# Four edits to a decoder kernel: a later load order in the second cross attention, causal rows scaled on ScalarE, a rotation-table wait moved, a zero fill issued in stage 1

## The reference, cut to what matters

```
x = layernorm(x + L0 self attention(x))             # 64 heads of 8, q, k, v with bias
x = layernorm(x + L0 cross attention(x, ctx))
x = layernorm(x + L0 mixture of experts(x))         # top 2 of 8 experts, on a latent of 256
x = layernorm(x + L1 causal attention(x))           # 16 heads of 128, 4 key/value heads, rotation
x = layernorm(x + L1 cross attention(x, ctx, pos))  # 32 heads of 16, rotation by position
x = layernorm(x + L1 ternary feed-forward(x))
def _layernorm(x, axis=-1, eps=1e-05):
    return (x - mean(x)) / sqrt(var(x) + eps)
```

## Time and profile before

| | us |
|---|---|
| median of 3 runs | 2950.88 |
| range of these | 2943.35 to 2951.95 |
| profiled execution, its own time | 2926.72 |
| its span | 2925.0 |
| TensorE busy | 2687.7 (92%) |
| VectorE busy | 1805.9 (62%) |
| ScalarE busy | 1409.8 (48%) |
| GpSimd busy | 316.3 (11%) |

### The profile page before, as it was taken

One profiled execution on the slowest core, in us unless ns is written; L12 is line 12 of the kernel. 1 busy time (PEld: TensorE's weight loads), 2 busy tenths in 40 slices (PEclk: granted clock), 3 DMA queues, 4 the chain that ended last, 5 costly groups with the idle time before them and its releaser, 6 DMA issues. The chain is left out here.

```text
span 2925.0 us, 40483 instructions
## 1 busy us (share of the span) xinstructions
PE 2687.7 (92%) x12665; PEld 1678.4 (57%) x12686; DVE 1805.9 (62%) x3459; ACT 1409.8 (48%) x2965; POOL 316.3 (11%) x405
## 2 busy tenths in 40 slices
PE   8999997978999986998998999996999999997887
PEld 4454554445588863776776777774545454533443
DVE  5665674654443336755755756753777777874676
ACT  4454452322133322553652652742577676764554
POOL 0230003000711113001001001002110101000000
PEclk9999998989999998999999999998999999998999
DMA  4393104741687754223233223211000000002000
GB/s 151 71 108 80 43 14 152 275 154 49 202 273 242 241 181 163 95 102 103 72 107 111 66 101 115 66 65 58 5 5 6 5 6 2 2 2 87 8 22 29
DMA packets 114166, 266.24 MB, mean 91 GB/s; under 512 B 14464, under 2 KB 37008, under 8 KB 113200
## 3 DMA queue, kind: packets, MB, share of 16 engines
q1 hardware_dynamic: 97152, 211.16, 21.9%
q0 software_dynamic: 16816, 52.64, 7.9%
HBM read 208.97 MB, written 58.48 MB: 91 GB/s over the span
## 5 line engine op out<-in xcount | busy, mean ns | idle before, releaser
L2451 DVE TENSOR_REDUCE x_neg_max<-bank 128x1 f32<-128x512 f32 x512 | 327.4, 684 | 95.9 <-PE bank L2296 95.4
L2403 ACT ACTIVATE x_weights<-bank 128x512 f32<-128x512 f32 x512 | 279.1, 600 | 127.0 <-PE bank L2307 122.1
L1826 ACT ACTIVATE a_probs<-bank,a_neg_max 128x128 f32<-128x128 f32 (+3 forms) x256 | 135.9, 531 | 241.7 <-DVE a_neg_max L1916 237.6
L1726 PE MATMUL bank<-a_x_high,a_weights 128*128 128x512 f32 x640 | 219.2, 406 | 9.2 <-DVE a_x_low L1848 4.5
L109 PEld LDWEIGHTS bank<-all_ident,a_probs 128*128 128x128 f32 x1200 | 151.4, 140 | 84.2 <-issue 44.7
L109 PE MATMUL bank<-all_ident,a_probs 128*128 128x128 f32 x1200 | 193.4, 273 | 2.2 <-ACT a_probs_t L1818 2.2
L1761 PE MATMUL bank<-a_k_cols,a_q_cols 128*128 128x128 f32 (+3 forms) x512 | 176.8, 434 | 0.3
L1818 ACT COPY a_probs_t<-bank 128x128 f32<-128x128 f32 (+3 forms) x256 | 107.4, 420 | 144.2 <-PE bank L109 144.0
L1790 PE MATMUL bank<-a_wo,a_att_high 128*128 128x512 f32 x512 | 162.3, 398 | 4.7 <-DVE a_q_cols L1865 2.9
L1451 DVE TENSOR_TENSOR moe_acc<-bank,moe_acc 128x512 f32 x79 | 54.6, 692 | 170.7 <-PE bank L1117 170.5
L1106 PE MATMUL bank<-moe_gh_cols,moe_item 128*128 128x256 f32 x632 | 151.9, 384 | 2.5 <-DMA moe_item<-moe_items 2.2
(11 more groups left out here) (407 smaller groups left out, 5538.4 us busy)
## 6 DMA issues: line engine op xcount, KB each, us to landing
a_weights<-split_qkv SPq DMA_DIRECT2D x80, 512.0 KB, 3.6
moe_item<-moe_items SPq DMA_DIRECT2D x79, 257.0 KB, 3.6
moe_item<-moe_items SPq DMA_DIRECT2D x79, 256.0 KB, 3.5
a_wo<-split_out SPq DMA_DIRECT2D x8, 2048.0 KB, 7.9
a_wo<-split_out SPq DMA_DIRECT2D x16, 1024.0 KB, 10.2
split_qkv<-x_qkv_parts SPq DMA_DIRECT2D x12, 1024.0 KB, 5.6
moe_items<-in_L_ffn_e_w POOLq DMA_DIRECT2D x40, 256.0 KB
split_out<-a_turned SPq DMA_DIRECT2D x8, 1024.0 KB, 4.4
```

The costliest lines, as they stand in the source:

```text
L1726: last = pe.matmul(mm[g % 2], weight[:, k, :], x[:, k, :], start=n == 0, stop=n == 3 * KD - 1)
L1826: act.activation(probs[:, n % SLOTS, 0:t], sc[n % 4][:, 0:t], ACT.Exp, bias=neg_max[:, n:n + 1], accum_out=row_sum[:, n:n + 1]).then_inc(s ...
L2403: act.activation(weights[:, chunk % 2, k, :], weight_banks[slot % 2], ACT.Exp).then_inc(s.weight.free, 1)
L2451: dve.tensor_reduce(neg_max[:, g % 2, j, h:h + 1], score_banks[slot % 3], AX.X, ALU.max, negate=True) \
```

## The change

It has four parts. (1) In `cross_attention_1` the second context half's turn for unit 0 moves from -0.95 to 2.8 in the order, behind the first q projection's `rope_swap`; and SP issues wout and bout after the second context half. (2) In `self_attention_1` POOL's two 128x2048 instructions are gone; ACT waits for shift and does the same in four Identity activations over 128x512. (3) The two waits at the start of DVE's block stand inside the batch, after the first batch's `low_x`. (4) The zero fill is issued by POOL in `self_attention_0`, behind `pack_experts` and ahead of the rstd loop, and no more in `cross_attention_0`.

```diff
--- self_attention_0, POOL
             layernorm_rstd(pool, st, 0, m, s)
             pack_experts(pool, packed, a)
+            pool.memset(zeros[:], 0.0).then_inc(s.zeros_made, 1)
+            pool.wait_ge(s.zeros_made, 1)
+            pool.dma_start(packed.sorted.rearrange("(t p) d -> p t d", p=P), zeros[:].unsqueeze(1).to_broadcast([P, packed.sorted_tiles, LATENT])) \
+                .then_inc(packed.cleared, 16)
             with pool.Fori(1, B) as b:
                 layernorm_rstd(pool, st, b, m, s)
+            pool.wait_ge(packed.cleared, 16)
--- cross_attention_0, POOL
+            pool.memset(next_w.w2[:, ALL:, :], 0.0)
             pool.memset(next_w.router[:], 0.0).then_inc(zeros_made, 1)
-            pool.memset(next_w.w2[:, ALL:, :], 0.0)
-            pool.memset(zeros[:], 0.0).then_inc(zeros_made, 1)
-            pool.wait_ge(zeros_made, 2)
+            pool.wait_ge(zeros_made, 1)
             load_moe_weights(pool, next_w, a)
-            pool.dma_start(packed.sorted.rearrange("(t p) d -> p t d", p=P), zeros[:].unsqueeze(1).to_broadcast([P, SUB * TILES, LATENT])) \
-                .then_inc(packed.cleared, 16)
             for b in range(B):
                 layernorm_rstd(pool, st, b, m, s)
-            pool.wait_ge(packed.cleared, 16)
--- self_attention_1, ACT (end of a batch), DVE (start), POOL (end of a batch)
+                act.wait_ge(s.shift_made, b + 2)
+                for j in range(NT):
+                    x = m.x_tok[:, b * NT + j, :]
+                    act.activation(x, x, ACT.Identity, bias=shift[:, j:j + 1], scale=st.rstd[:, j:j + 1])
...
-            dve.wait_ge(tables_loaded, 16)
-            dve.wait_ge(s.made, 2)
             def low_x(b):
...
             def batch(b, last_one):
+                dve.wait_ge(tables_loaded, 16)
+                dve.wait_ge(s.made, 2)
...
                 pool.tensor_tensor(shift[:], neg_mean[:], st.rstd[:], ALU.mult).then_inc(s.shift_made, 1)
-                pool.drain()
-                x = m.x_tok[:, bass.ds(b * NT, NT), :]
-
-                def per_row(v):
-                    return v.unsqueeze(2).to_broadcast([P, NT, D])
-
-                pool.tensor_tensor(x, x, per_row(st.rstd[:]), ALU.mult)
-                pool.drain()
-                pool.tensor_tensor(x, x, per_row(shift[:]), ALU.add)
--- cross_attention_1, order and SP
-    WEIGHTS_AT, VALUES_AT, COPY_AT, BACK_AT, TURN_AT, CONTEXT_AT = -1.929, 1.112, 1.113, 2.282, 0.434, -0.95
+    WEIGHTS_AT, VALUES_AT, COPY_AT, BACK_AT, TURN_AT, LATE_CONTEXT_AT = -1.929, 1.112, 1.113, 2.282, 0.434, 2.8
...
-            for half, late in enumerate((-1, CONTEXT_AT)):
+            for half, late in enumerate((-1, LATE_CONTEXT_AT)):
                 turn(at + late, ("c", 0, half))
...
             sp.dma_start(wkv[:], chunked(Wkv)).then_inc(w_kv, 16)
-            sp.dma_start(wout[:], chunked(Wout)).then_inc(w_out, 16)
-            sp.dma_start(bout_row[:], bout.partition_broadcast(P)).then_inc(w_out, 16)
             for piece in order:
                 if piece[0] == "evac" and piece[1][0] == "c":
                     _, b, half = piece[1]
                     if (b, half) != (B - 1, 1):
                         sp.wait_ge(*filled(piece[1]))
                         load_context(*((b, 1) if half == 0 else (b + 1, 0)))
+                    if (b, half) == (0, 0):
+                        sp.dma_start(wout[:], chunked(Wout)).then_inc(w_out, 16)
+                        sp.dma_start(bout_row[:], bout.partition_broadcast(P)).then_inc(w_out, 16)
```

More of the change, by code:

```diff
@@ L168, in self_attention_0 @@
         feats, feats_t = sb("feats", [P, NT, D]), x_cols
+        zeros = sb("zeros", [P, LATENT])
         out_rows = [whole[:], high[:].bitcast(F32)]
@@ L177, in self_attention_0 @@
         s.var_ready, s.rstd_ready = sem("var_ready"), sem("rstd_ready")
+        s.zeros_made = sem("zeros_made")
         s.out_rows_in, s.out_high, s.out_low, s.out_stored = (sem(n) for n in ("out_rows_in", "out_high", "out_low", "out_stored"))
@@ L445, in cross_attention_0 @@
         probs, probs_t = sb("probs", [P, 2, NT, S]), sb("probs_t", [P, NT, S])
-        zeros, zeros_made = sb("zeros", [P, LATENT]), sem("zeros_made")
+        zeros_made = sem("zeros_made")
         qkv_rows, qkv_parts = sb("qkv_rows", [P, 2, KD, 2 * HD1]), sb("qkv_parts", [P, 2, 2, 2, KD, HD1], F32R)
@@ L711, in __init__ @@
         self.sorted = nc.dram_tensor("moe_sorted", (TILES * TOKENS, LATENT), F32, kind="Internal").ap()
+        self.sorted_tiles = SUB * TILES
         self.mixed = nc.dram_tensor("moe_mixed", (SPARE * TOKENS, LATENT), F32, kind="Internal").ap()
```

## The result

| | us |
|---|---|
| before, median of 4 | 2950.43 (2943.35 to 2951.95) |
| changed, median of 4 | 2918.80 (2914.56 to 2921.30) |
| ratio | 0.9907, 95% interval 0.9890 to 0.9924 |
| changed, profiled execution | 2918.93, span 2917.2 |

The account below looks back on a forecast made before the run. TensorE, busy 92% of the span, was taken as the bound, so only its stops count. Terms -6.8 - 4.5 - 10.2 - 2.2 - 1.3 + 6.6 = -18.4 us gave a median of 2932.5 us, range 2920 to 2946.

Parts of the forecast that it names:

- Second cross attention: Start of that stage: q half 0 no longer waits for the second context half; first pad 6.8 us earlier, bounds 4 to 7.5.
- the sum: All terms added: -18.4 us, giving 2908.3 for the profiled execution and 2932.5 for the median.
- Stage end: End of the causal stage: ScalarE's four steps replace POOL's instructions behind shift; gain 4.5 us, bounds 3 to 4.6.
- Boundaries: Causal stage's three batch boundaries: POOL's instruction no longer holds the rotation's addition; gain 10.2 us, bounds 5 and 14.
- Tables' wait: Start of the causal stage: first low parts no longer wait for rotation tables; gain 2.2 us, bounds 0.5 to 3.8.
- no new stop: Start of the causal stage: the values' weight still lands 1.4 us before TensorE, started 2.2 us earlier, wants it.
- Zero fill: Removed from first cross attention: gain 1.3 us, bounds 0 and 3; added in stage 1: loss 6.6, bounds 0 and 8.
- The hold: Stage 1: POOL's fill issue waits until its queue empties, starts at 250.9, delays rstd; TensorE stands 5.2 us.
- A: Rival: the fill's issue is not held in stage 1, term 0; sum -25.0, 2925.9 us; chance 0.14.
- C: Rival: causal boundaries gain nothing, the 3.8 us coming from the loop's turn, not POOL; -8.2, 2942.7 us; chance 0.07.
- D: Rival, slower: zero fill holds POOL until landed, TensorE idle 29.4 us in stage 1; +6.1, 2957 us; chance 0.05.
- B: Rival: context half lands as late as now, half the boundary gain returns as waits; about 2941 us; chance 0.17.

Follow-up runs that it names:

- before again: The unchanged kernel run once more for a second trace, no edit, against itself in the same rounds: 2945.69 us against 2946.31, ratio 1.0000.
- scratch runs: Kernel before with causal rows on ScalarE, plus GpSimd multiplying or memsetting an unused tile at each batch's end: 2923.86 and 2918.53 us, before 2930.78.
- part 3 alone: Kernel before with only the rotation tables' wait moved behind the first low parts: 2927.78 us against 2929.82, ratio 0.9993.

## Why the prediction was right, and where it was off

- *Second cross attention, 6.8 us.* The mechanism came as written: wq, then the bank, the context turn between. The size was low: the first pad is 8.9 us earlier and not 7.0, the first score 10.8 us earlier than in the trace of before (48.95 to 38.2). In eight traces without part 1 the stage took 686 to 690 us, in five with parts 1 and 2 it took 677 to 680: 9 us. Of the 1.9 us at the pad 1.7 are wq: it landed 9.1 us behind the stage's first DMA in the trace that the sum was made from and 7.4 here, so TensorE stood 1.98 us for it and not 3.4. The other 1.9 us up to the first score are clock: 0.85 of full between pad and score in that trace, 1.00 here. Neither is the edit's doing: before again had 7.4 and 1.00 too, and against it the first score is 7.8 us earlier.
- *Stage end, 4.5 us.* Shift to next stage 3.2 us, 3.3 predicted; it was 7.8. Right.
- *Boundaries, 10.2 us.* The cause was right and the scratch runs show it. From shift to the next batch's first score product the three boundaries took 27.9, 28.6 and 23.8 us in the trace of before and 24.2, 25.3 and 19.5 in the changed one: 11.2 us less, of which 4.2 at the third (4.0 predicted, with the clock). That the first two boundaries always stop TensorE 6.2 us was wrong: in four of five further traces one of them was about 3 us already. The causal stage without part 2 took 855.7 to 861.7 us, with it (and no scratch work) 839.9 to 844.6: some 16 us, to which stage end, boundaries and the tables' wait contribute; predicted 16.9.
- *Tables' wait, 2.2 us.* The stop is 1.57 us and not 3.82, as predicted, but "no new stop" was wrong: TensorE then stood for the weights, 1.51 us in the changed kernel and 1.33 and 2.30 with part 3 alone. Some 1 us is left.
- *Zero fill, -1.3 and +6.6 us.* This is the term that failed: 5.3 us of loss together, where the first two stages came out 4.9 us shorter. These 10.2 us are most of what the sum fell short by, 13.2 by the medians. The kernel was still forecast faster since the other terms, which came near, are larger. The hold itself came as written: in all 14 traces the issue started 1.7 to 3.1 us behind the last packet of GpSimd's own queue (1.7 in each of the ten where it stands in the first cross attention; at 243.68, 240.62, 258.93 and 259.92 in the others). Whether it waits for an empty queue, or for room that is there only then, no run tells. The price failed: I took one trace's 249.2 for the queue's last packet, which came at 241.5 in the changed kernel, at 238 to 247 in the first rounds and at 254 to 262 in the later ones. It cost nothing with the issue at 240.62 and 243.68, and some 2 us at 258.93, since in those rounds TensorE too started late. Missing was 3 us at the end of stage 1, less 1 at the end of the next, from GpSimd's drains.
- *The sum.* Measured again, the same change gained 21.2 us, much nearer to 18.4; the two intervals (22 to 32 us, 14 to 29) overlap. So how far the sum was off is itself uncertain.
- *Rivals.* A and C fell: the issue is held, and the 3.8 us are GpSimd's. D did not occur; rstd ran right behind the issue. Of B the context half landed 10.7 us behind the stage's first DMA (15.7 before), and at the boundaries no stop came back; the one that did is that of the weights above.
- *The own time of the profile.* I saw that the profiled execution lay 24 us below the median and carried the sum over. It did no harm, since the missing stops are in a stage that the change leaves alone.

The Trainium skill ("Perfetto Trace Analysis", "DMA Instruction — SWDGE (GPSIMD)") states only that DMA engines may start on an instruction's descriptors before GpSimd has written the last of them. That GpSimd would therefore begin this issue behind 60 unfinished DMAs was the prediction's own conclusion, and the traces contradict it: the issue at 243.68 began 75.69 us after GpSimd was free.

## What to carry to other kernels

An engine at 11% busy can still be the bound of single instructions of another: look for the maximum beside the median of each line. Set a DMA from GpSimd behind the small steps that others wait for, and a drain where GpSimd is idle, ahead of a stage's end; here the traces show the stops at both stage ends shrink, which the times do not tell from noise. When a wait is taken away, look at what would be waited for next. Before summing small terms from one profile, compare its own time with the median, stage by stage with a second trace if there is one.

## What the runs showed of the hardware that I had not expected

- GpSimd's drain at the end of a block took 5.9 us after 60 DMAs, 4.1 after the weight loads of the first cross attention (part 4), and 7.7 in the mixture stage, and 0.9 where a held issue had come in between.
- The mixture stage took 532 to 538 us in nine traces and 558 to 561 in five, by starts on VectorE and ScalarE that came up to 15.0 us late for something the profile calls remote; its cause is open.
- The last packet of the same packing DMAs left GpSimd's queue between 238 and 247 us in the four traces of the first rounds and between 254 and 262 in the eight later ones.
- At the start of the second cross attention the granted clock between first pad and first score was 1.00 in nine traces and 0.73 to 0.85 in five; the stop ahead of the stage was 8.2 to 14.0 us in the former and 8.2 to 12.9 in the latter.
